# One transformer layer on eight cores: LayerNorm's small operations, a buffer of half the width, and a scheduler that weighs ScalarE's table loads more

## The chip, the cores and the metric

The kernel runs on all 8 cores of one Trainium2 chip. Each core does the same program on its own sequence (batch element) of 4096 tokens by 1024 features; the cores exchange nothing. The metric is the device time of the slowest core in microseconds (us). The kernel before took 1746.99 us, the median of three runs from 1746.04 to 1747.79.

A core has engines that run at the same time and wait for each other by semaphores: TensorE (PE) multiplies 128x128 blocks into eight PSUM banks, VectorE (DVE) and ScalarE (ACT) do elementwise work, GpSimd (POOL) does little here, and SyncE (SP) starts the transfers of x and y. Each engine takes its own instructions strictly in the order in which the program has them.

## What is computed

LN is LayerNorm without weights. Everything is along the 4096 tokens of one sequence:

```python
def attn(x):                                  # x = LN(input)
    xc = causal_depthwise_conv(x, conv_weight, conv_bias)     # 4 taps
    r = sigmoid(xc @ Wr.T + Wr_b);  i = sigmoid(xc @ Wi.T + Wi_b)
    a = power(sigmoid(log_a), 8 * r)
    b = sqrt(clip(1 - a * a, 1e-6)) * (i * xc)
    logA = clip(cumsum(log(clip(a, 1e-7))), -80)              # over tokens
    h = exp(logA) * cumsum(b * exp(-logA))                    # over tokens
    return rmsnorm(h @ out_w.T, norm_w)
def ffn(x):                                   # x = LN(input)
    xr = mu_r * x + (1 - mu_r) * x_prev;  xk = mu_k * x + (1 - mu_k) * x_prev
    return sigmoid(xr @ W_r.T) * (square(relu(xk @ W_k.T)) @ W_v.T)
x = x + LN(attn(LN(x)))
x = x + LN(ffn(LN(x)))
```

## The kernel before

**Chunks.** The tokens are worked in 16 chunks of 256. The first half of a chunk (F) loads it (L336), normalises it (statistics L443 to L475, L495), transposes it (L511, evacuated by ScalarE at L518), does the convolution as matmuls with diagonal matrices (L544, bias L553, evacuated L561), and computes the two gates: 64 matmuls with w_wr and 64 with w_wi (L586), each group of 8 into one PSUM bank, evacuated with Sigmoid (L595). The second half (B) of a chunk is the recurrence and the feed-forward part. In the program's loop the second half of chunk c-1 is emitted around the first half of chunk c, so that both stand in one period.

**The recurrence (B1).** z = r times a constant (L614, VectorE); la = max(z, clip) (L633); ScalarE computes exp(2z) (L637); VectorE clips it (L641); ScalarE takes sqrt(1 - that) (L653); VectorE scans la over the tokens in eight instructions (L666), adds the carry and clips (L678, eight), multiplies i by xc (L619) and that by the root (L657); ScalarE computes exp(-logA) (L688) and exp(logA) (L709); VectorE multiplies (L691), scans again (L700, eight) and forms h (L718, eight). Then h goes through w_ow (L758, 32 matmuls).

**The feed-forward part (B2).** Behind w_ow come RMS norm, LayerNorm, the residual (L770 to L825), the third LayerNorm (L841), transposes (L857, L864), the token mix (L883 to L899), r = Sigmoid(w_fr) (L919 matmuls, L927 ScalarE), k = Relu(w_fk) (L950 matmuls, L960 ScalarE), its square (L968, VectorE), w_fv (L988, 32 matmuls), the product with r (L996, VectorE, reads PSUM), the fourth LayerNorm, the residual (L1026), the store of y, and, behind that store on the same queue, the load of the chunk that reuses this input buffer.

**Buffers.** There are pools of buffers of 128x2048 elements: five of fp32 (`p32`) and six of bf16 (`p16`); a buffer is taken from a ring in the order of emission, and its new writer waits until its old readers are done. In listings both are shown as p. Six PSUM banks (PS) are taken in turn in the same way: a bank's next matmul group waits until ScalarE or VectorE has read the last one. PT is a seventh and eighth bank for transposes.

**What sets the order.** The program first emits all operations with their dependences and an estimated length, then `schedule()` lays them out with a list scheduler on estimated times. An operation's priority is the longest estimated path behind it, and of the ready operations of an engine the one with the highest priority goes first. On ScalarE `pick_scalar` takes up to 6 ready operations and adds TBL_NS (1283) to the priority of those whose table set is the one loaded: Exp and Ln are one set, Sigmoid another, Sqrt a third; Copy, Square and Relu run in any. The order that comes out is fixed in the program; on the chip no engine changes it.

## Time and profile before

| what | value |
|---|---|
| median of three runs | 1746.99 us |
| the profiled execution | 1742.71 us |
| its span, slowest core (core 1) | 1741.2 us (cores: 1720.7 to 1741.2) |
| PE busy | 983.3 us, 56% |
| DVE busy | 944.7 us, 54% |
| ACT busy | 816.4 us, 47% |
| the chain that ended last, by engine | PE 40%, DVE 24%, ACT 17%, issue 15% |
| mean granted TensorE clock, core 1 | 0.778 of full speed |

No engine is busy for more than 56% of the span. The chain that ended last follows the work backwards from the last instruction to what released it each time; it runs through three engines, so that the time is set by how they wait for each other. Busy shares are means over a period of some 102 us that repeats 15 times. Each line of a listing of instructions has its start in us from the start of the span, its length, the engine, the line of the kernel, output and input, the shape and how many were merged (xN), and in square brackets how long the engine had been idle and what released it.

### The profile page before, as it was taken

The numbers are of one execution on the slowest core, as the hardware profiler recorded it, in microseconds if no ns is written. First come the engines' busy times: TensorE is split into PE (matmuls) and PEld (weight loads), VectorE is DVE, ScalarE is ACT, GpSimd is POOL, SyncE is SP. The second block draws the span as 40 slices with busy tenths as digits, with TensorE's granted clock in tenths as the row PEclk, the third lists the DMA queues.
The fourth block names the chain that finished last, engine by engine and source line by source line (L and its number), as shares of the span: only waits on it lengthen the run. The fifth ranks groups of instructions, "written<-read, shape, count | busy, mean of one in ns | idle before, by whom it ended". The sixth has DMA issues, their size and how long they took to land.

```text
span 1741.2 us, 20480 instructions; the slowest of 8 cores (1720.7 to 1741.2 us)
## 1 busy us (share of the span) xinstructions
PE 983.3 (56%) x5762; PEld 595.8 (34%) x5762; DVE 944.7 (54%) x1570; ACT 816.4 (47%) x1303; POOL 30.8 (2%) x57
## 2 busy tenths in 40 slices
PE   0345737464664747467484656838465673846525
PEld 0133415142442515244251433416143341514313
DVE  0145565565456565555655555565555556555552
ACT  0554635354563535446354544635364463545422
POOL 1000000000000000000000000000000000000000
PEclk9977969687886867778686776868697786867867
DMA  9650010101001010000101000010100001010000
GB/s 131 123 85 1 1 49 1 49 1 39 10 1 49 1 49 1 31 19 1 49 1 49 1 25 25 1 49 1 49 1 25 25 1 49 1 48 1 1 24 25
DMA packets 21360, 47.49 MB, mean 27 GB/s; under 512 B 6912, under 2 KB 6912, under 8 KB 21248
## 3 DMA queue, kind: packets, MB, share of 16 engines
q1 hardware_dynamic: 14944, 33.59, 5.7%
q0 software_dynamic: 6304, 12.59, 4.8%
q8 instruction: 48, 0.79, 0.2%
q14 instruction: 64, 0.52, 0.1%
HBM read 41.99 MB, written 16.78 MB: 34 GB/s over the span
## 4 chain that ended last, share of the span: by engine, by line
PE 40%; DVE 24%; ACT 17%; issue 15%; SPq 2%; DMA 1%; DVEq 1%; ACTq 1%
PE PS L586 10%; PE PS L758 8%; PE PS L988 8%; PE PS L544 5%; DVE p L700 5%; PE PS L950 5%; ACT p L595 4%; DVE p L718 4%; ACT p L960 2%; DVE p L614 2%; DVE xin L1026 2%; ACT p L637 2%; ACT PS L455 2%; ACT p L709 2%; DVE vout L1019 2%
## 5 line engine op out<-in xcount | busy, mean ns | idle before, releaser
L758 PE MATMUL PS<-w_ow,p 128*128 128x512 bf16 x512 | 141.2, 444 | 331.8 <-DVE p L718 305.6
L758 PEld LDWEIGHTS PS<-w_ow,p 128*128 128x128 bf16 x512 | 56.8, 111 | 416.2 <-issue 373.0
L988 PE MATMUL PS<-w_fv,p 128*128 128x512 bf16 x512 | 150.0, 463 | 76.3 <-DVE p L968 43.5
L455 ACT ACTIVATE PS<-xin 128x1024 f32<-128x1024 f32 x64 | 65.8, 1028 | 263.7 <-DMA xin<-x 204.6
L544 PE MATMUL PS<-ln1F,diag 128*128 128x256 bf16 x512 | 108.6, 386 | 126.6 <-ACT stats L472 104.6
L586 PE MATMUL PS<-p,w_wi 128*128 128x256 bf16 x1024 | 149.2, 298 | 51.9 <-ACT p L595 51.7
L586 PE MATMUL PS<-p,w_wr 128*128 128x256 bf16 x1024 | 143.4, 305 | 25.8 <-ACT p L595 23.4
L919 PE MATMUL PS<-w_fr,p 128*128 128x512 bf16 x512 | 136.3, 391 | 9.9 <-DVE p L893 7.0
L586 PEld LDWEIGHTS PS<-p,w_wi 128*128 128x128 bf16 x1024 | 106.5, 106 | 95.1 <-issue 70.4
L586 PEld LDWEIGHTS PS<-p,w_wr 128*128 128x128 bf16 x1024 | 110.1, 109 | 56.2 <-issue 33.3
L950 PE MATMUL PS<-p,w_fk 128*128 128x256 bf16 x1024 | 123.4, 275 | 5.6 <-ACT p L595 3.2
L544 PEld LDWEIGHTS PS<-ln1F,diag 128*128 128x128 bf16 x512 | 65.1, 132 | 165.0 <-issue 142.0
L988 PEld LDWEIGHTS PS<-w_fv,p 128*128 128x128 bf16 x512 | 57.6, 114 | 168.6 <-issue 133.1
L950 PEld LDWEIGHTS PS<-p,w_fk 128*128 128x128 bf16 x1024 | 100.1, 99 | 28.2 <-issue 8.9
L614 DVE TENSOR_TENSOR p<-p,c_loga 128x2048 f32<-128x2048 bf16 x16 | 36.7, 2293 | 129.6 <-ACT p L595 129.6
L666 DVE TENSOR_TENSOR_SCAN p<-p,zeros 128x256 f32<-128x256 f32 x128 | 88.5, 692 | 13.6 <-DVE p L666 0.5
L700 DVE TENSOR_TENSOR_SCAN p<-p,zeros 128x256 f32<-128x256 bf16 x128 | 88.5, 692 | 13.2
L595 ACT ACTIVATE p<-PS,c_wrb 128x256 bf16<-128x256 f32 x128 | 60.7, 474 | 73.2 <-PE PS L586 64.1
L968 DVE TENSOR_TENSOR p<-p 128x2048 bf16<-128x2048 bf16 x16 | 19.6, 1225 | 118.3 <-ACT p L960 76.1
L770 ACT ACTIVATE vout<-PS 128x512 f32<-128x512 f32 x64 | 38.2, 597 | 75.4 <-PE PS L758 72.5
L595 ACT ACTIVATE p<-PS,c_wib 128x256 bf16<-128x256 f32 x128 | 60.7, 474 | 25.4 <-PE PS L586 16.2
L919 PEld LDWEIGHTS PS<-w_fr,p 128*128 128x128 bf16 x512 | 51.1, 100 | 58.2 <-issue 20.8
(99 smaller groups left out, 1484.2 us busy)
## 6 DMA issues: line engine op xcount, KB each, us to landing
xin<-x SPq DMA_DIRECT2D x16, 1024.0 KB, 6.1
y<-xin SPq DMA_DIRECT2D x16, 1024.0 KB, 4.2
w_wr<-wr POOLq DMA_DIRECT2D x1, 2048.0 KB, 19.9
w_wi<-wi POOLq DMA_DIRECT2D x1, 2048.0 KB, 30.5
w_ow<-ow POOLq DMA_DIRECT2D x1, 2048.0 KB, 41.8
w_fr<-fr POOLq DMA_DIRECT2D x1, 2048.0 KB, 18.2
w_fk<-fk POOLq DMA_DIRECT2D x1, 2048.0 KB, 29.9
w_fv<-fv POOLq DMA_DIRECT2D x1, 2048.0 KB, 22.1
```

The lines of the kernel that those rows point to most:

```text
L455: lambda e, s2=s, b=b, S_=S_, xap=xap, base=base: e.activation(bank2(b), xap[:, s2, :], AF.Square, bias=0.0, scale=1.0, accum_out=S_[:, ba ...
L544: lambda e, b=b, ch=ch, kk=kk, half=half: e.matmul(PS[:, b * 512 + half * CH: b * 512 + half * CH + CH], diag[:, ch * 4 + kk, :], ln1F[:, ...
L586: lambda e, b=b, wn=wn, k=k, m=m, xcF=xcF: e.matmul(bank(b, CH), wsb[wn][:, k, m * 128:(m + 1) * 128], feat(xcF)[:, k, :], start=(k == 0), ...
L595: lambda e, b=b, gb=gb, m=m, biasn=biasn: e.activation(feat(gb)[:, m, :], bank(b, CH), AF.Sigmoid, bias=cols[biasn][:, m:m + 1], scale=1.0),
L614: lambda e, z=z, r16=stt["r16"], bc=lnsig_bc: e.tensor_tensor(feat(z), feat(r16), bc, ALU.mult),
L666: lambda e, m=m, cb=cbuf, la=la: e.tensor_tensor_scan(feat(cb)[:, m, :], feat(la)[:, m, :], zeros32[:, :], 0.0, ALU.add, ALU.add),
L700: lambda e, m=m, S2=Ssc, t=tbuf: e.tensor_tensor_scan(feat(S2)[:, m, :], feat(t)[:, m, :], zeros32[:, :], 0.0, ALU.add, ALU.add),
L718: lambda e, m=m, h=hF, A=Abuf, S2=Ssc: e.scalar_tensor_tensor(feat(h)[:, m, :], feat(S2)[:, m, :], carryS[:, m:m + 1], feat(A)[:, m, :], A ...
L758: lambda e, b=b, k=k, s=s, half=half, hF=hF: e.matmul(bank(b), feat(hF)[:, k, s * 128:(s + 1) * 128], wsb["ow"][:, k, half * 512:(half + 1 ...
L919: lambda e, b=b, k=k, s=s, half=half, xr=xrF: e.matmul(bank(b), feat(xr)[:, k, s * 128:(s + 1) * 128], wsb["fr"][:, k, half * 512:(half + ...
L950: lambda e, b=b, k=k, m=m, half=half, xk=xkF: e.matmul(PS[:, b * 512 + half * CH: b * 512 + half * CH + CH], wsb["fk"][:, k, m * 128:(m + ...
L988: lambda e, b=b, k=k, s=s, half=half, ka=kaF: e.matmul(bank(b), feat(ka)[:, k, s * 128:(s + 1) * 128], wsb["fv"][:, k, half * 512:(half + ...
```

## The change

Four edits go together:

1. **LayerNorm statistics.** Before, the sum of squares was divided by D in its own VectorE instruction (L463) and the square of the mean subtracted from it in another (L469). Now one scalar_tensor_tensor does both.
2. **Table weight.** `pick_scalar` looks at 10 ready operations in place of 6 and gives 2600 in place of 1283 to those of the loaded set. The price of a load in the scheduler's own clock (TBL_NS) stays.
3. **Buffers.** Four fp32 and eight bf16 buffers in place of five and six: the same memory.
4. **r in bf16.** The result of L927, which L996 reads, is written to a bf16 buffer.

The other switches in the diff (PT1) are off and change nothing.

```diff
@@ -21,11 +21,13 @@
 SUB = CH // 128
 NXIN = int(os.environ.get("K_NXIN", "2"))
 NST = int(os.environ.get("K_NST", "4"))
-N_P32 = int(os.environ.get("K_P32", "5"))
-N_P16 = int(os.environ.get("K_P16", "6"))
+N_P32 = int(os.environ.get("K_P32", "4"))
+N_P16 = int(os.environ.get("K_P16", "8"))
 N_VOUT = int(os.environ.get("K_VOUT", "1"))
 BANK_MODE = os.environ.get("K_BANKS", "global")
 PT_ROLE = os.environ.get("K_PTROLE", "0") == "1"
+PT1 = os.environ.get("K_PT1", "0") == "1"
+RF16 = os.environ.get("K_RF16", "1") == "1"
 HOPX = float(os.environ.get("K_HOP", "250"))
 SQ2 = os.environ.get("K_SQ", "0") == "1"
 XFG = os.environ.get("K_XFG", "0") == "1"
@@ -56,6 +58,8 @@
 
 
 TBL_NS = 1283.0
+TBL_BONUS = float(os.environ.get("K_TBLNS", "2600"))
+TBL_WIN = int(os.environ.get("K_TBLWIN", "10"))
 COLD_IDLE = 800.0
 COLD_WIN = 3400.0
 
@@ -133,12 +137,12 @@
 
         def pick_scalar():
             tmp = []
-            while ready["scalar"] and len(tmp) < 6:
+            while ready["scalar"] and len(tmp) < TBL_WIN:
                 tmp.append(heapq.heappop(ready["scalar"]))
             best_key, best_adj = None, None
             for key in tmp:
                 op = self.all[key[-1]]
-                adj = -key[0] + (TBL_NS if (op.afn and op.afn == cur_tbl) else 0.0)
+                adj = -key[0] + (TBL_BONUS if (op.afn and op.afn == cur_tbl) else 0.0)
                 if best_adj is None or adj > best_adj:
                     best_adj, best_key = adj, key
             for key in tmp:
@@ -265,7 +269,7 @@
 
     sch = Sched()
     if BANK_MODE == "global":
-        banksF = banksM = banksB = Banks(0, 6)
+        banksF = banksM = banksB = Banks(0, 7 if PT1 else 6)
     else:
         banksF = Banks(0, 2)
         banksM = Banks(2, 2)
@@ -310,8 +314,8 @@
         vouts = [sb("vout%d" % i, [128, SUB * D], F32) for i in range(N_VOUT)]
         p32 = Pool([sb("p32_%d" % i, [128, SUB * D], F32) for i in range(N_P32)])
         p16 = Pool([sb("p16_%d" % i, [128, SUB * D], BF16) for i in range(N_P16)])
-        PS = st.enter_context(nc.psum_tensor("PS", [128, 3072], F32))
-        PT = st.enter_context(nc.psum_tensor("PT", [128, 2048], BF16))
+        PS = st.enter_context(nc.psum_tensor("PS", [128, 3584 if PT1 else 3072], F32))
+        PT = st.enter_context(nc.psum_tensor("PT", [128, 1024 if PT1 else 2048], BF16))
         tb_free = [[], []]
 
         def bank(b, n=512):
@@ -460,15 +464,13 @@
             tm_ = sch.emit("vector", lambda e, S_=S_, base=base: e.tensor_single_scalar(
                 S_[:, base + 4:base + 4 + SUB], S_[:, base:base + SUB], 1.0 / D, ALU.mult),
                 deps=t1, est=150)
-            te2 = sch.emit("vector", lambda e, S_=S_, base=base: e.tensor_single_scalar(
-                S_[:, base + 6:base + 6 + SUB], S_[:, base + 2:base + 2 + SUB], 1.0 / D, ALU.mult),
-                deps=tsq, est=150)
             tmm = sch.emit("vector", lambda e, S_=S_, base=base: e.tensor_tensor(
                 S_[:, base + 8:base + 8 + SUB], S_[:, base + 4:base + 4 + SUB], S_[:, base + 4:base + 4 + SUB], ALU.mult),
                 deps=[tm_], est=150)
-            tq = sch.emit("vector", lambda e, S_=S_, base=base: e.tensor_tensor(
-                S_[:, base + 8:base + 8 + SUB], S_[:, base + 6:base + 6 + SUB], S_[:, base + 8:base + 8 + SUB], ALU.subtract),
-                deps=[te2, tmm], est=150)
+            tq = sch.emit("vector", lambda e, S_=S_, base=base: e.scalar_tensor_tensor(
+                S_[:, base + 8:base + 8 + SUB], S_[:, base + 2:base + 2 + SUB], 1.0 / D,
+                S_[:, base + 8:base + 8 + SUB], ALU.mult, ALU.subtract),
+                deps=tsq + [tmm], est=150)
             tln = sch.emit("scalar", lambda e, S_=S_, base=base: e.activation(
                 S_[:, base + 14:base + 14 + SUB], S_[:, base + 8:base + 8 + SUB], AF.Ln, bias=LN_EPS, scale=1.0),
                 deps=[tq], est=250, afn="exp")
@@ -503,7 +505,7 @@
             tok_tr1 = []
             tok_ev1 = []
             for s2 in range(SUB):
-                tb = 0 if PT_ROLE else s2
+                tb = 0 if (PT1 or PT_ROLE) else s2
                 trs_ = []
                 for j in range(KC):
                     trs_.append(sch.emit(
@@ -849,7 +851,7 @@
             tok_evF = []
             tok_trF = []
             for s2 in range(SUB):
-                tb = 1 if PT_ROLE else s2
+                tb = 0 if PT1 else (1 if PT_ROLE else s2)
                 trs_ = []
                 for j in range(KC):
                     trs_.append(sch.emit(
@@ -904,7 +906,7 @@
                 "gpsimd", lambda e: e.tensor_copy(fF[:, :, 0:1], fF[:, :, CH:CH + 1]),
                 deps=[tok_d] + tok_xr + tok_xk + [glob["tok_tailF"]], est=400)
 
-            rf32, rfdep = p32.take()
+            rf32, rfdep = (p16.take() if RF16 else p32.take())
             tok_rf = []
             all_wr = []
             for s in range(SUB):
@@ -1004,7 +1006,7 @@
                     tok_vo.append(te)
                     banksB.give(ids, [te])
             p16.give(kaF, all_wv)
-            p32.give(rf32, tok_vo)
+            (p16 if RF16 else p32).give(rf32, tok_vo)
 
             acc4 = stats[:, ps, 64:64 + 2 * SUB].rearrange("p (a b) -> p a b", b=2)
             t1d = sch.emit("vector", lambda e, S_=S_, acc4=acc4: e.tensor_tensor(
```

The rows below are the programs' orders. The changed kernel's line numbers are 4 higher than before up to the LayerNorm statistics (L460 is L464) and 2 higher behind them (L586 is L588, L614 is L616); between, L466 is L467 and L469 is L470. A name such as p_3 is buffer 3 of one of the pools. All periods from the second to the last but one have the same rows but for the numbers of buffers and banks.

TensorE, in one period, from the transposes of the third LayerNorm (L857) to the first w_fk matmuls, before:

```order
L857 MATMUL PT<-ident,p_5 128x128 x16
L586 MATMUL PS<-p_3,w_wr 128x256 x64
L586 MATMUL PS<-p_3,w_wi 128x256 x26
L919 MATMUL PS<-w_fr,p_5 128x512 x2
L586 MATMUL PS<-p_3,w_wi 128x256 x4
L919 MATMUL PS<-w_fr,p_5 128x512 x2
L586 MATMUL PS<-p_3,w_wi 128x256 x2
L919 MATMUL PS<-w_fr,p_5 128x512 x11
L586 MATMUL PS<-p_3,w_wi 128x256 x10
L919 MATMUL PS<-w_fr,p_5 128x512
L586 MATMUL PS<-p_3,w_wi 128x256 x22
L950 MATMUL PS<-p_1,w_fk 128x256 x52
```

and in the changed kernel, the stretch with the last w_wr matmuls:

```order
L588 MATMUL PS<-p_3,w_wi 128x256 x2
L588 MATMUL PS<-p_3,w_wr 128x256 x2
L921 MATMUL PS<-w_fr,p_7 128x512 x2
L588 MATMUL PS<-p_3,w_wi 128x256 x2
L588 MATMUL PS<-p_3,w_wr 128x256 x2
L588 MATMUL PS<-p_3,w_wi 128x256 x2
L588 MATMUL PS<-p_3,w_wr 128x256 x2
L921 MATMUL PS<-w_fr,p_7 128x512 x2
L588 MATMUL PS<-p_3,w_wi 128x256 x2
L588 MATMUL PS<-p_3,w_wr 128x256 x2
L588 MATMUL PS<-p_3,w_wi 128x256 x4
L952 MATMUL PS<-p_0,w_fk 128x256
```

The gate matmuls with w_wr and w_wi stood one behind the other; now they are mixed two by two, with w_fr among them. Ahead of the last w_wr matmul stand 64 w_wr before, and 64 w_wr, 44 w_wi and 16 w_fr now.

ScalarE, from the first gate evacuation to the last Exp of the recurrence, before:

```order
L595 ACTIVATE p_5<-PS,c_wrb 128x256 x8
L595 ACTIVATE p_1<-PS,c_wib 128x256 x2
L637 ACTIVATE p_2<-p_1 128x2048
L595 ACTIVATE p_1<-PS,c_wib 128x256 x2
L927 ACTIVATE p_4<-PS 128x512 x2
L595 ACTIVATE p_1<-PS,c_wib 128x256 x4
L709 ACTIVATE p_1<-p_3 128x2048
L960 ACTIVATE p_1<-PS 128x512 x4
L927 ACTIVATE p_4<-PS 128x512 x2
L653 ACTIVATE p_3<-p_2 128x2048
L688 ACTIVATE p_5<-p_3 128x2048
```

and now, from the fifth w_wr evacuation on (ahead of these stand four of w_wr and two of w_wi):

```order
L597 ACTIVATE p_1<-PS,c_wrb 128x256 x2
L597 ACTIVATE p_5<-PS,c_wib 128x256 x2
L929 ACTIVATE p_2<-PS 128x512 x2
L597 ACTIVATE p_1<-PS,c_wrb 128x256 x2
L597 ACTIVATE p_5<-PS,c_wib 128x256 x2
L639 ACTIVATE p_1<-p_2 128x2048
L597 ACTIVATE p_5<-PS,c_wib 128x256 x2
L655 ACTIVATE p_6<-p_1 128x2048
L962 ACTIVATE p_1<-PS 128x512 x4
L929 ACTIVATE p_2<-PS 128x512 x2
L690 ACTIVATE p_7<-p_0 128x2048
L711 ACTIVATE p_1<-p_0 128x2048
```

The Sqrt (L653, now L655) has moved ahead of the Relu evacuations; Exp(logA) (L709, now L711), which stood ahead of them, is the last, behind Exp(-logA) (L688, now L690), with no other set between. The sets loaded in a period change seven times before and six times now.

VectorE, from z to the square of k, before:

```order
L614 TENSOR_TENSOR p_0<-p_1,c_loga 128x2048
L896 TENSOR_TENSOR p_1<-p_2,c_muk 128x2048
L899 TENSOR_TENSOR p_1<-p_1,fF 128x2048
L633 TENSOR_SCALAR p_1<-p_0 128x2048
L641 TENSOR_SCALAR p_3<-p_3 128x2048
L666 SCALAR_TENSOR_TENSOR p_4<-p_1,zeros 128x256 x8
L672 COPY ctmp<-p_4 128x8
L678 TENSOR_SCALAR p_4<-p_4,carryC 128x256
L619 TENSOR_TENSOR p_4<-p_0,p_3 128x2048
L678 TENSOR_SCALAR p_4<-p_4,carryC 128x256 x7
L683 TENSOR_TENSOR carryC<-carryC,ctmp 128x8
L968 TENSOR_TENSOR p_3<-p_0 128x2048
```

and now:

```order
L898 TENSOR_TENSOR p_0<-p_6,c_muk 128x2048
L901 TENSOR_TENSOR p_0<-p_0,fF 128x2048
L616 TENSOR_TENSOR p_2<-p_1,c_loga 128x2048
L635 TENSOR_SCALAR p_3<-p_2 128x2048
L643 TENSOR_SCALAR p_1<-p_1 128x2048
L668 SCALAR_TENSOR_TENSOR p_0<-p_3,zeros 128x256 x3
L621 TENSOR_TENSOR p_4<-p_5,p_3 128x2048
L668 SCALAR_TENSOR_TENSOR p_0<-p_3,zeros 128x256 x5
L674 COPY ctmp<-p_0 128x8
L970 TENSOR_TENSOR p_5<-p_1 128x2048
L680 TENSOR_SCALAR p_0<-p_0,carryC 128x256 x8
```

The mix for w_fk (L896, L899) now stands ahead of z. The square of k (L968, now L970) stands ahead of the eight carry additions (L678, now L680) and no longer behind them.

VectorE, around the product with r, before:

```order
L657 TENSOR_TENSOR p_4<-p_5,p_4 128x2048
L691 TENSOR_TENSOR p_4<-p_4,p_1 128x2048
L996 SCALAR_TENSOR_TENSOR vout,stats<-PS,p_2 128x512 x4
L1010 TENSOR_TENSOR stats<-stats 128x2
L460 TENSOR_SCALAR stats<-stats 128x2
L463 TENSOR_SCALAR stats<-stats 128x2
L466 TENSOR_TENSOR stats<-stats 128x2
L469 TENSOR_TENSOR stats<-stats 128x2
L700 SCALAR_TENSOR_TENSOR p_2<-p_4,zeros 128x256
L1019 TENSOR_SCALAR vout<-vout,stats 128x1024 x2
L1026 TENSOR_TENSOR xin<-xin,vout 128x2048
L700 SCALAR_TENSOR_TENSOR p_2<-p_4,zeros 128x256 x7
```

and now:

```order
L659 TENSOR_TENSOR p_4<-p_6,p_4 128x2048
L693 TENSOR_TENSOR p_4<-p_4,p_7 128x2048
L702 SCALAR_TENSOR_TENSOR p_2<-p_4,zeros 128x256 x2
L998 SCALAR_TENSOR_TENSOR vout,stats<-PS,p_2 128x512 x4
L1012 TENSOR_TENSOR stats<-stats 128x2
L464 TENSOR_SCALAR stats<-stats 128x2
L467 TENSOR_TENSOR stats<-stats 128x2
L470 SCALAR_TENSOR_TENSOR stats<-stats 128x2
L702 SCALAR_TENSOR_TENSOR p_2<-p_4,zeros 128x256
L1021 TENSOR_SCALAR vout<-vout,stats 128x1024 x2
L1028 TENSOR_TENSOR xin<-xin,vout 128x2048
L702 SCALAR_TENSOR_TENSOR p_2<-p_4,zeros 128x256 x5
```

Two of the eight second scans (L700, now L702) stand ahead of the product L998, and the LayerNorm statistics have three instructions instead of four, with one instead of three behind ScalarE's squares.

## Rows read from the trace of the kernel before

**Rows 1.** By stage: length; PE, PEld, DVE, ACT, POOL busy (instructions); PE clock; DMA share, GB/s:

```profile
1456.00:1464.50 8.50, 8.47 (x36) 3.73 (x37) 4.89 (x9) 3.40 (x11) 0.00 (x0) 0.83 0.00 0
1464.50:1486.00 21.50, 11.56 (x72) 7.48 (x70) 10.55 (x27) 12.41 (x27) 0.22 (x1) 0.61 0.01 2
1486.00:1528.40 42.40, 32.34 (x227) 22.90 (x224) 24.16 (x28) 23.81 (x33) 1.22 (x1) 0.90 0.00 1
1528.40:1538.30 9.90, 9.77 (x32) 3.62 (x32) 2.92 (x3) 6.77 (x5) 0.00 (x0) 0.72 0.00 0
1538.30:1558.60 20.30, 0.01 (x1) 0.04 (x1) 16.53 (x33) 3.74 (x8) 0.00 (x0) 0.56 0.29 103
```

**Rows 2.** TensorE's instructions in time, first w_ow of the program:

```profile
137.91 8.73 PE L758 MATMUL PS<-w_ow,p 128*128 128x512 bf16 x32 [26.20 <-DVE stats L463]
```

**Rows 3.** TensorE's instructions in time, last w_ow of the program:

```profile
1660.84 8.44 PE L758 MATMUL PS<-w_ow,p 128*128 128x512 bf16 x32 [20.36 <-DVE p L718]
```

**Rows 4.** Who waited for whom: us in total, times, longest:

```profile
PE PS L758 <- DVE p L718: 305.6, 15, 20.6
```

**Rows 5.** ScalarE's table loads (112, six groups): busy us, mean ns | idle before:

```profile
L595 ACT ACT_TABLE_LOAD x32 | 41.1, 1283 | 28.7 <-PE PS L586 27.3
...
L709 ACT ACT_TABLE_LOAD x15 | 19.2, 1283 | 89.6 <-DVE p L678 89.6
```

**Rows 6.** ScalarE's instructions in time, gate stage of that period:

```profile
1501.78 1.28 ACT L637 ACT_TABLE_LOAD   x1 [1.46 <-DVE p L614]
1503.07 1.91 ACT L637 ACTIVATE p<-p 128x2048 f32<-128x2048 f32 x1
...
1520.17 1.28 ACT L709 ACT_TABLE_LOAD   x1 [6.25 <-DVE p L678]
...
1523.46 2.67 ACT L960 ACTIVATE p<-PS 128x512 bf16<-128x512 f32 x4
...
1527.50 1.29 ACT L927 ACTIVATE p<-PS 128x512 f32<-128x512 f32 x2
```

**Rows 7.** ScalarE's instructions in time, when the next x has come:

```profile
1557.57 1.03 ACT L455 ACTIVATE PS<-xin 128x1024 f32<-128x1024 f32 x1 [13.80 <-DMA xin<-x]
```

**Rows 8.** VectorE's instructions in time, same period:

```profile
1499.35 2.29 DVE L614 TENSOR_TENSOR p<-p,c_loga 128x2048 f32<-128x2048 bf16 x1 [6.46 <-ACT p L595]
...
1508.14 6.25 DVE L666 TENSOR_TENSOR_SCAN p<-p,zeros 128x256 f32<-128x256 f32 x8
...
1526.98 1.23 DVE L968 TENSOR_TENSOR p<-p 128x2048 bf16<-128x2048 bf16 x1 [6.68 <-ACT p L960]
...
1537.84 0.69 DVE L996 SCALAR_TENSOR_TENSOR vout<-PS,p 128x512 f32<-128x512 f32 x1 [1.09 <-PE PS L988]
...
1545.86 2.29 DVE L1026 TENSOR_TENSOR xin<-xin,vout 128x2048 f32<-128x2048 f32 x1
1548.25 5.46 DVE L700 TENSOR_TENSOR_SCAN p<-p,zeros 128x256 f32<-128x256 bf16 x7
1553.83 4.61 DVE L718 SCALAR_TENSOR_TENSOR p<-p,carryS,p 128x256 bf16<-128x256 f32 x8
```

**Rows 9.** TensorE's instructions in time, first gate matmuls of that period:

```profile
1486.05 4.28 PE L586 MATMUL PS<-p,w_wr 128*128 128x256 bf16 x22
...
1492.07 4.64 PE L586 MATMUL PS<-p,w_wr 128*128 128x256 bf16 x41 [0.30 <-ACT p L595]
```

**Rows 10.** TensorE's instructions in time, its wait in the gates, and on:

```profile
1506.97 0.37 PE L586 MATMUL PS<-p,w_wi 128*128 128x256 bf16 x1 [2.67 <-ACT p L595]
...
1520.66 2.75 PE L919 MATMUL PS<-w_fr,p 128*128 128x512 bf16 x12
1528.47 9.77 PE L988 MATMUL PS<-w_fv,p 128*128 128x512 bf16 x32 [5.05 <-DVE p L968]
```

**Rows 11.** VectorE's groups by line: count | busy us, mean ns | idle before:

```profile
L678 DVE TENSOR_SCALAR p<-p,carryC 128x256 f32<-128x256 f32 x128 | 45.2, 353 | 15.9 <-DVE p L678 2.8
...
L463 DVE TENSOR_SCALAR stats<-stats 128x2 f32<-128x2 f32 x64 | 10.8, 169 | 52.1 <-ACT PS L455 50.6
```

## The prediction

> **What bounds the kernel now.** I read the shares of the page first: no engine is busy for more than 56% of the span, so no sum of busy times gives the end. The chain of waits runs through three engines. The table by stage shows a period of 102.6 us in five stages [rows 1]: w_ow on TensorE (8.5), a stage of norms and convolution (21.5), gates, w_fr and w_fk (42.4), w_fv (9.9), and 20.3 us in which TensorE does nothing and VectorE is busy for 16.5. The list of waits names that last gap: TensorE waited for h (L718) 15 times, 305.6 us in all [rows 4]. From the first to the last w_ow there are 15 periods, (1660.84 - 137.91)/15 = 101.5 us each [rows 2, 3]; whatever shortens a period counts 15 times.
>
> Within a period I then read the timelines of the three engines, from the gates on [rows 6, 8 to 10]. z (L614) starts at 1499.35, when w_wr's eight banks are evacuated. The first scans (L666) start at 1508.14 and the carry additions (L678) end at 1520.0, for on ScalarE the load for Exp(logA) (L709) starts at 1520.17. The Relus (L960) stand behind it and start at 1523.46, though the w_fk matmuls were done at 1520.6 (there the last twelve of w_fr start). Behind them the square (L968) comes at 1526.98, w_fv at 1528.47, and the product L996 at 1537.84, 9.37 us into w_fv. From L996 VectorE works almost without a break to the end of L718 at 1558.44. So two things decide a period: when L996 can start, and how much VectorE still has to do after it.
>
> **The change part by part.** Times are in that period, as if all ahead of the gates stayed.
>
> *Gates.* The first TensorE matmuls go as before: 22 in 4.28 us, 0.195 each, then at the higher rate 41 in 4.64 us, 0.113 each [rows 9]; a 512-column matmul takes 0.23 (2.75/12) [rows 10] and counts as two units. At 1492.07 some 28 of the new order are done (26 of w_wr and two of w_wi, whose banks came free at the same moment as now). The last w_wr is number 64 + 44 + 2x16 = 140. 112 units x 0.113 = 12.7, so it ends at 1504.7. ScalarE then has two evacuations of w_fr and two of w_wr, 2.1 us with their gaps: z starts at 1507.05, **7.7 us later** than before.
>
> *From z to the scans.* Before, the mix for w_fk (3.5 us and gaps) stood between z and L633; it now lies in VectorE's wait ahead of z and costs nothing. Then z 2.29, load 1.28 and Exp 1.91 on ScalarE [rows 6], the clip 1.23, hops of 0.15 to 0.2 each: the scans start at 1514.25, 6.1 later than before. Eight scans with L619 among them and L672 take 6.25 + 1.33 + 0.28 and gaps, to 1522.2.
>
> *w_fk.* Before, TensorE waited 2.67 us at unit 126 for ScalarE, which was inside Exp(2z) and its two loads, and went on at 1506.97 [rows 10]. In the new order a like wait (the banks of the last w_wr and w_wi) comes at unit 145 and ends near 1508.1, with some 150 done where the old order had 131. That is 19 units, 2.2 us: w_fk ends at 1518.4 in place of 1520.6.
>
> *ScalarE.* After Exp(2z), a load and two w_wi evacuations the Sqrt takes 1.28 + 1.91 to 1518.4; the Relus follow at once, to 1521.3, as nothing of L709 (1.28 + 1.91) stands ahead of them. w_fr's evacuations with their load end at 1524.0.
>
> *Square and w_fv.* L968 starts behind the scans at 1522.3 and ends at 1523.5; w_fv needs also w_fr's last bank: it starts at 1524.1, 4.3 earlier. Its 9.37 us to the first product give 1533.5.
>
> *VectorE up to the product.* The eight carry additions, 8 x 0.35 and gaps 3.7 [rows 11], end at 1527.3; load and Exp(-logA) to 1530.6; L691 and two scans to 1533.7. So VectorE and TensorE arrive together, and L996 starts at 1533.8, **4.0 us earlier**. Exp(logA) runs beside it. The two engines are within 0.3 us of each other: half a gain on one is no gain.
>
> *After the product.* Two of eight scans are done already: 2 x 0.8 = **1.6** (5.46 for seven, and gaps) [rows 8]. The LayerNorm: of three instructions behind ScalarE's squares one is left, the other moves into the wait; 2 x 0.27 = **0.5** (0.17 each and the gap) [rows 11]. No row has a scalar_tensor_tensor of two columns; L996, of 512, takes 0.69, at most what it costs [rows 8], and at least the 0.17 of the tensor_scalar. Nearest in size is the latter, which I take. In the other three LayerNorms of a period the same 0.5 lies beside other work of ScalarE or TensorE (the transpose's evacuation, the convolution, the first part of w_ow) and I count nothing; without that cover it would be 0.5 x 3 more gained, not lost.
>
> *r in bf16.* ScalarE writes 512 columns in 0.6 to 0.7 us as bf16 (L960, 2.67 for four) and as fp32 (L927, 1.29 for two) alike [rows 6]. VectorE's scans with a bf16 input take 5.46 for seven against 6.25 for eight in fp32, the same each [rows 8]. So nothing; the bounds are 0.1 either way for four products.
>
> *The table load.* The 112 loads of 1.28 us [rows 5] become some 97; of the one saved per period the worth is already in the above, since L709 no longer stands ahead of the Relus.
>
> *The buffers.* With four fp32 buffers Exp(logA) must write where the Sqrt read. That is why the Sqrt has to come first; it stands first, so no wait is left of it.
>
> *The x transfer.* The store of y goes out at the end of L1026 (1548.15) and x is there at 1557.57, 9.4 later [rows 7, 8]. Five scans and h are 8.7 us now, so the first norm's statistics wait for x 0.7 us more; w_ow (8.4 us) covers that and the statistics with about 1 us left.
>
> Sum: 4.0 + 1.6 + 0.5 = 6.1 in this period. It is one of the better: where TensorE's clock stays low for longer after its wait, w_fk ends later and the gain is nearer to 5. I take 5.5 x 15 = 82. The first chunk, with its Sqrt ahead of six w_wi evacuations, may lose 1.7; the last one, with three LayerNorms in the open, gains 1.6. From the profiled execution's 1742.7: 1660.7. The median of the runs is 4.3 above that execution, so 1665.
>
> Here a rule speaks about price. From the end of the Relus (1526.13) to the start of w_fr's evacuation (1527.50) the rows show 1.37 us, with one load of 1.28 in it [rows 5, 6]. The Trainium skill, ScalarE: Activation LUTs, section What ACT_TABLE_LOAD costs, adds a drain of about 1380 ns to each switch, 2.66 us in all; by it the load taken from ahead of the Relus would be worth 1.4 us more a period, about 20 us more in all. The trace does not agree, and I leave it out.
>
> **Rivals.** *z is later still.* The mixing of w_wi into w_wr is paid in z. If TensorE's clock falls in the mixed stretch (the low level costs 0.195 in place of 0.113 a matmul), 40 units at it put z 3.3 us later, VectorE decides alone, and a period gains 2.8: 42 in all, 1705. For it: VectorE is already on the edge. Against it: the same matmuls ran at 0.113 for 41 in a row [rows 9].
>
> *The x transfer becomes the bound.* The margin is some 1 us. If the transfer takes 2.5 us longer against other cores' traffic, since it starts under more load, a period loses 1.5 of its 5.5: 60 in all, 1687.
>
> *The order of before was the better.* The square now stands in VectorE's queue ahead of the carry additions. If w_fk ended late, it would hold them, Exp(-logA) and the scans. Its place is L968, its price each us that w_fk is late. From w_fk's end to the product it takes 15.1 us now and took 17.2 before (1537.84 - 1520.6); with the 2.1 after the product the change loses only if w_fk ends over 4.2 us later than before. Twice the wait of 2.67 and 20 units more at the low rate (1.6) would do that just about; at 5 us late it is 0.8 x 15 = 12 slower, 1759. Nothing in the rows shows it.
>
> *Only the loads count.* If the reordering cancels itself and only 0.5 us of the norm is won in a period, it is 8 us, 1739.
>
> **How the numbers follow.** The forecast, a gain of 4.5 to 6.5 a period, 0.58; z later 0.16; the x transfer 0.10; nearly nothing won 0.09, a third of it within 0.2%; slower 0.04; a clock that stays high in more places, a gain of 7 to 8 a period, 1635, 0.03. The range: below, the last case and a w_fk end that lets 7 us be won; above, z later with its 1705 and a little more. 1638 to 1708. A difference under 0.2% (3.5 us) can't be told from none with this kernel. Faster 0.93, within 0.2% 0.03, slower 0.04.
>
> **What would show it.** In the profile after: z should start some 7 to 8 us later in the period than now; VectorE's wait ahead of the square should be nearly gone; w_fv should begin about 4 us earlier and wait for w_fr's last bank or the square; the first product should find two scans done; Exp(logA) should run with no load ahead of it; loads should number some 97; TensorE's wait for h should fall from 20.35 to about 18.5. The prediction is wrong if the gates' stage does not end earlier, or if w_ow begins to wait for x or for buffers; if the span falls by less than 40 us, the step on z is the first to suspect.

## The result, and the profile after

The changed kernel takes 1641.87 us (median; 1635.57 to 1643.55) where the kernel before took 1745.43 in the same comparison: a ratio of 0.9401, 95% interval 0.9387 to 0.9416, 103.6 us less. Measured again on another chip it was 1638.65 us against 1742.2, 0.9406 (0.9386 to 0.9426). The forecast was 1665 with a range of 1638 to 1708; the time came out 23 us below it, 4 us above the range's lower end.

The page of the changed kernel: the span, busy times, and the shares of the chain that ended last.

```profile
span 1640.9 us, 19943 instructions; the slowest of 8 cores (1627.7 to 1640.9 us)
...
PE 947.8 (58%) x5762; PEld 583.2 (36%) x5762; DVE 934.2 (57%) x1506; ACT 795.9 (49%) x1287; POOL 15.7 (1%) x57
...
PE 34%; DVE 32%; ACT 15%; issue 13%; SPq 2%; DMA 1%; DVEq 1%; ACTq 1%
```

VectorE has come up to TensorE, and in the chain of waits it has nearly TensorE's share. By stage, the period that begins at 992.15, with the columns of [rows 1]:

```profile
992.00:1000.50 8.50, 8.35 (x32) 3.57 (x33) 4.91 (x9) 4.08 (x10) 0.00 (x0) 0.82 0.01 2
1000.50:1022.20 21.70, 11.82 (x74) 7.77 (x73) 10.21 (x25) 12.56 (x27) 0.23 (x1) 0.61 0.00 0
1022.20:1059.40 37.20, 30.87 (x226) 22.36 (x224) 21.29 (x20) 24.05 (x33) 0.22 (x1) 0.95 0.01 1
1059.40:1068.20 8.80, 8.75 (x32) 3.48 (x32) 5.66 (x11) 5.20 (x4) 0.00 (x0) 0.81 0.00 0
1068.20:1088.00 19.80, 0.09 (x1) 0.10 (x1) 16.27 (x31) 2.71 (x7) 0.00 (x0) 0.55 0.27 106
```

Four of the five stages are within 1.1 us of those before. The gates' stage is 37.2 us in place of 42.4, with TensorE granted 0.95 of its clock in place of 0.90. TensorE's timeline of that period shows a part of it: the one wait of 2.67 us in the gates of [rows 10] has become three short ones, here 0.95 and two of 0.30 (only the first is shown). All waits from the first gate matmul to w_fk's end are 2.5 us in place of 5.1. Then come the last of w_fr, w_fv, and w_ow of the next period; below them the last w_ow of the program, which answers to [rows 3].

```profile
1042.16 0.27 PE L588 MATMUL PS<-p,w_wi 128*128 128x256 bf16 x1 [0.95 <-ACT p L597]
...
1052.90 2.75 PE L921 MATMUL PS<-w_fr,p 128*128 128x512 bf16 x12
1059.44 8.75 PE L990 MATMUL PS<-w_fv,p 128*128 128x512 bf16 x32 [3.79 <-DVE p L970]
1087.91 8.43 PE L760 MATMUL PS<-w_ow,p 128*128 128x512 bf16 x32 [19.72 <-DVE p L720]
```

```profile
1559.15 10.02 PE L760 MATMUL PS<-w_ow,p 128*128 128x512 bf16 x32 [16.99 <-DVE p L720]
```

From the first w_ow (139.13) to the last are 15 periods in 1420.0 us, 94.67 each, against 101.53 before [rows 2, 3]: 6.86 x 15 = 103 us, the whole gain. The list of waits answers to [rows 4]:

```profile
PE PS L760 <- DVE p L720: 290.4, 15, 20.1
```

290.4/15 = 19.4 us a period in place of 20.4, where the prediction had 18.5. VectorE's timeline from z on, to be read beside [rows 8]:

```profile
1042.76 2.29 DVE L616 TENSOR_TENSOR p<-p,c_loga 128x2048 f32<-128x2048 bf16 x1 [9.99 <-ACT p L597]
...
1048.56 1.23 DVE L643 TENSOR_SCALAR p<-p 128x2048 f32<-128x2048 f32 x1 [2.18 <-ACT p L639]
1049.89 2.28 DVE L668 TENSOR_TENSOR_SCAN p<-p,zeros 128x256 f32<-128x256 f32 x3
...
1057.95 1.22 DVE L970 TENSOR_TENSOR p<-p 128x2048 bf16<-128x2048 bf16 x1 [0.21 <-DVE ctmp L674]
...
1066.37 1.22 DVE L693 TENSOR_TENSOR p<-p,p 128x2048 bf16<-128x2048 bf16 x1 [2.18 <-ACT p L690]
1067.70 1.49 DVE L702 TENSOR_TENSOR_SCAN p<-p,zeros 128x256 f32<-128x256 bf16 x2
1069.29 0.69 DVE L998 SCALAR_TENSOR_TENSOR vout<-PS,p 128x512 f32<-128x512 f32 x1
...
1073.87 0.16 DVE L470 SCALAR_TENSOR_TENSOR stats<-stats 128x2 f32<-128x2 f32 x1 [0.66 <-ACT PS L459]
...
1083.15 4.62 DVE L720 SCALAR_TENSOR_TENSOR p<-p,carryS,p 128x256 bf16<-128x256 f32 x8
1088.15 2.29 DVE L447 TENSOR_REDUCE stats<-xin 128x2 f32<-128x2048 f32 x1 [0.39 <-DMA xin<-x]
```

z (L616) has a wait of 9.99 us ahead of it; the square (L970), which waited 6.68, waits 0.21; the product (L998) has no wait ahead of it. The end of L720 releases w_ow. From z to the end of L720 VectorE has two more waits of 2.18 us for ScalarE, which then works on what VectorE has just made (Exp(2z) and Exp(-logA)), and one of 0.66. So the chain from z on is VectorE's own work with these stops. x is there at 1088.1, 0.2 us after w_ow has begun. ScalarE, beside [rows 6]:

```profile
1045.18 1.28 ACT L639 ACT_TABLE_LOAD   x1 [1.46 <-DVE p L616]
...
1052.17 1.91 ACT L655 ACTIVATE p<-p 128x2048 bf16<-128x2048 f32 x1
1054.17 2.67 ACT L962 ACTIVATE p<-PS 128x512 bf16<-128x512 f32 x4
...
1058.21 1.29 ACT L929 ACTIVATE p<-PS 128x512 bf16<-128x512 f32 x2
...
1066.29 1.91 ACT L711 ACTIVATE p<-p 128x2048 f32<-128x2048 f32 x1
```

The Sqrt (L655) comes first, the Relus (L962) follow it, and Exp(logA) (L711) has no load ahead. Of loads there are 99: 32 by L597, 16 each by L639, L655, L690 and L929, and three at the program's ends (the 112 of before leave those three out). Three of the groups, beside [rows 5]:

```profile
L597 ACT ACT_TABLE_LOAD x32 | 41.1, 1283 | 26.8 <-PE PS L588 25.4
...
L655 ACT ACT_TABLE_LOAD x16 | 20.5, 1283 | 5.5 <-DVE p L621 3.0 <-DVE p L643 1.5
L690 ACT ACT_TABLE_LOAD x16 | 20.5, 1283 | 50.4 <-DVE p L680 50.4
```

To compare kernels I read the same moments off the timelines of each of the core that the profile shows and took means over periods 2 to 14 (us; "gates" is the first gate matmul, "product" the first L996 or L998). The runs of the experiments stand in the same table:

```
                    w_ow to  gates   w_fk end  gates    gates to  product to  period
                    gates    to z    (from g.) to w_fv  product   next w_ow
before              29.51    13.05   34.59     42.13    51.31     20.77       101.59
after               29.22    20.03   30.57     36.87    46.70     18.70        94.63
e1_ln_only          29.26    13.30   34.80     42.20    51.61     20.45       101.32
e2_buf_only         29.02    20.25   30.55     36.96    46.89     19.27        95.18
e3_tbl_old          28.78    20.03   30.57     36.83    46.67     18.70        94.15
e4_p16_6            28.74    12.92   35.68     41.84    50.70     17.98        97.42
e6_delay            29.12    20.15   30.57     36.92    46.82     18.70        94.63
e7_wr_first         37.87    13.19   33.53     38.93    47.72     17.04       102.63
e8_residual_pool    37.76    19.82   30.73     36.75    46.46     20.27       104.49
e9_wr_first_head    29.06    13.12   33.28     38.90    47.78     17.09        93.92
e10_head_only       36.65    20.33   30.63     37.12    47.00     18.67       102.32
e11_norm_scalar     28.54    20.24   30.60     37.01    46.91     18.07        93.52
e12_both            29.26    13.30   33.24     39.03    47.90     16.50        93.66
```

### The profile page after: what moved, and what is told of

It is laid out like the page before. It is cut to its first block, busy times and chain, and to the rows that moved or that the text cites. A ratio compares the mean times of both kernels' runs of the same rounds, so it can differ in the third digit from the quotient of the medians.

```text
span 1640.9 us, 19943 instructions; the slowest of 8 cores (1627.7 to 1640.9 us)
## 1 busy us (share of the span) xinstructions
PE 947.8 (58%) x5762; PEld 583.2 (36%) x5762; DVE 934.2 (57%) x1506; ACT 795.9 (49%) x1287; POOL 15.7 (1%) x57
## 4 chain that ended last, share of the span: by engine, by line
PE 34%; DVE 32%; ACT 15%; issue 13%; SPq 2%; DMA 1%; DVEq 1%; ACTq 1%
PE PS L588 11%; PE PS L760 9%; PE PS L546 6%; DVE p L702 5%; DVE p L668 5%; DVE p L720 4%; PE PS L921 4%; DVE p L680 3%; ACT p L597 2%; DVE xin L1028 2%; DVE p L616 2%; ACT p L690 2%; ACT p L639 2%; DVE vout L1021 2%; ACT PS L459 2%
## 5 line engine op out<-in xcount | busy, mean ns | idle before, releaser
L760 PE MATMUL PS<-w_ow,p 128*128 128x512 bf16 x512 | 147.1, 459 | 320.5 <-DVE p L720 290.4
L588 PE MATMUL PS<-p,w_wi 128*128 128x256 bf16 x1024 | 182.2, 274 | 33.8 <-ACT p L597 33.6
L588 PE MATMUL PS<-p,w_wr 128*128 128x256 bf16 x1024 | 179.3, 301 | 3.7 <-ACT p L563 2.4
L990 PE MATMUL PS<-w_fv,p 128*128 128x512 bf16 x512 | 143.5, 449 | 62.9 <-DVE p L970 53.0
L546 PE MATMUL PS<-ln1F,diag 128*128 128x256 bf16 x512 | 103.9, 373 | 126.1 <-ACT stats L474 120.7
L952 PE MATMUL PS<-p,w_fk 128*128 128x256 bf16 x1024 | 141.8, 275 | 9.0 <-ACT p L597 5.5
L616 DVE TENSOR_TENSOR p<-p,c_loga 128x2048 f32<-128x2048 bf16 x16 | 36.7, 2293 | 176.1 <-ACT p L597 176.1
L588 PEld LDWEIGHTS PS<-p,w_wi 128*128 128x128 bf16 x1024 | 99.4, 98 | 73.6 <-issue 46.5
L588 PEld LDWEIGHTS PS<-p,w_wr 128*128 128x128 bf16 x1024 | 109.4, 108 | 33.4 <-issue 4.8
L597 ACT ACTIVATE p<-PS,c_wrb 128x256 bf16<-128x256 f32 x128 | 60.7, 474 | 74.0 <-PE PS L588 66.4
L702 DVE TENSOR_TENSOR_SCAN p<-p,zeros 128x256 f32<-128x256 bf16 x128 | 88.6, 692 | 13.9 <-DVE p L702 0.9
L447 DVE TENSOR_REDUCE stats<-xin 128x2 f32<-128x2048 f32 x16 | 36.6, 2286 | 61.1 <-DMA xin<-x 61.0
L720 DVE SCALAR_TENSOR_TENSOR p<-p,carryS,p 128x256 bf16<-128x256 f32 x128 | 62.0, 484 | 14.6 <-DVE p L702 0.7
L597 ACT ACTIVATE p<-PS,c_wib 128x256 bf16<-128x256 f32 x128 | 60.7, 474 | 11.6 <-PE PS L588 1.2
```

Of the source, the lines that this page charges most:

```text
L546: lambda e, b=b, ch=ch, kk=kk, half=half: e.matmul(PS[:, b * 512 + half * CH: b * 512 + half * CH + CH], diag[:, ch * 4 + kk, :], ln1F[:, ...
L588: lambda e, b=b, wn=wn, k=k, m=m, xcF=xcF: e.matmul(bank(b, CH), wsb[wn][:, k, m * 128:(m + 1) * 128], feat(xcF)[:, k, :], start=(k == 0), ...
L597: lambda e, b=b, gb=gb, m=m, biasn=biasn: e.activation(feat(gb)[:, m, :], bank(b, CH), AF.Sigmoid, bias=cols[biasn][:, m:m + 1], scale=1.0),
L616: lambda e, z=z, r16=stt["r16"], bc=lnsig_bc: e.tensor_tensor(feat(z), feat(r16), bc, ALU.mult),
L702: lambda e, m=m, S2=Ssc, t=tbuf: e.tensor_tensor_scan(feat(S2)[:, m, :], feat(t)[:, m, :], zeros32[:, :], 0.0, ALU.add, ALU.add),
L720: lambda e, m=m, h=hF, A=Abuf, S2=Ssc: e.scalar_tensor_tensor(feat(h)[:, m, :], feat(S2)[:, m, :], carryS[:, m:m + 1], feat(A)[:, m, :], A ...
```

## Experiments

Each ratio is to the kernel before on the same chip, with its 95% interval.

**Which part pays: e1 to e4.** The first takes the kernel before and changes the LayerNorm's variance alone.

```diff
-            te2 = ... tensor_single_scalar(S_[:, base+6..], S_[:, base+2..], 1.0 / D, ALU.mult)
-            tq = ... tensor_tensor(S_[:, base+8..], S_[:, base+6..], S_[:, base+8..], ALU.subtract)
+            tq = ... scalar_tensor_tensor(S_[:, base+8..], S_[:, base+2..], 1.0 / D,
+                     S_[:, base+8..], ALU.mult, ALU.subtract)
```

> The kernel before with the LayerNorm edit alone; the order of all else stays. Theory (only the fourth LayerNorm of a period stands on the path, 2 x 0.27 us): about 0.53 x 15 = 8 us faster than before plus some 1.6 in the last chunk, 1745 to 1736, ratio 0.995. Rival (all four LayerNorms of a period stand on the path): 0.53 x 4 x 15 = 32 us, 1713. Rival (the new instruction costs what its neighbours saved): no change.

Measured: 1732.35 us, 0.9927 (0.9904 to 0.9949), 12.7 us less, where the expectation had some 10. Its 15 periods take 7.5 us less, 0.5 each, which is the number predicted, but in part by luck: behind the product, where the theory puts the gain, the table has 0.32 (20.45 for 20.77), and over all eight cores a period is 0.37 shorter. The last chunk, from the last w_ow on, is 4.1 us shorter (76.3 in place of 80.4), for 1.6 expected.

The second takes the kernel before with the buffers alone.

```diff
-N_P32 = 5; N_P16 = 6;  rf32, rfdep = p32.take()
+N_P32 = 4; N_P16 = 8;  rf32, rfdep = p16.take()
```

> The kernel before with the four fp32 and eight bf16 buffers and r in bf16, but the old LayerNorm and the old table weight. Theory (the buffers alone make the new order, the rest of the gain is theirs): changed kernel plus the LayerNorm's 9 to 10 us, 1642 + 9 = 1651. Rival (the table weight does a good part of it): 1665 or more, and seven loads a period.

Measured: 1646.1 us, 0.9427 (0.9406 to 0.9447). The first theory holds: the buffers alone bring the new order and 6.4 of the 7.0 us a period; the LayerNorm adds 0.57 behind the product (19.27 to 18.70).

The third takes the table edit out of the changed kernel: TBL_BONUS 1283 and TBL_WIN 6.

> The changed kernel with the table weight of before (6 ready operations, 1283). The steady periods come out in the same order. Theory (the table weight changes next to nothing here): 1642, within 2 us. Rival (it saves the load of each period, 1.28 us): 1642 + 19 = 1661.

Measured: 1629.86 us, 0.9338 (0.932 to 0.9355): faster than the changed kernel, whose two intervals it does not touch, and outside both expectations. e2 and e3 differ in the LayerNorm alone: 1646.1 and 1629.86, 16 us on the same chip. So of the change's parts the buffers give most, the LayerNorm 13 to 16 us, and with the table edit the kernel is some 11 us slower. The steady periods are ordered alike in e3 and the changed kernel. Two things differ. In the last chunk the larger weight lets one Relu stand behind w_fr's last evacuation, to save a load. ScalarE's timelines there, the changed kernel and then this one:

```profile
1610.59 1.98 ACT L962 ACTIVATE p<-PS 128x512 bf16<-128x512 f32 x3 [7.65 <-PE PS L952]
1613.29 1.29 ACT L929 ACTIVATE p<-PS 128x512 bf16<-128x512 f32 x2 [0.73 <-PE PS L921]
1614.67 0.60 ACT L962 ACTIVATE p<-PS 128x512 bf16<-128x512 f32 x1
```

```profile
1601.86 2.66 ACT L962 ACTIVATE p<-PS 128x512 bf16<-128x512 f32 x4 [7.65 <-PE PS L952]
1604.62 1.29 ACT L929 ACTIVATE p<-PS 128x512 bf16<-128x512 f32 x2
```

The last twelve w_fr matmuls start at 1610.60 and at 1601.87; with the Relu held back w_fv starts 6.32 us behind that, without it 4.31, and the first product 14.38 and 11.32. So the table edit costs 3.1 us in the last chunk: 2.0 by w_fv's later start, 1.1 by w_fv itself, whose 32 matmuls take 8.46 us in place of 7.07 (81.8 us from the last w_ow on in the changed kernel, 76.4 here; the other 2.3 are w_ow and w_fr at different clocks). The second part lies in the lengths of single periods: the 15 of them take 1409.2 us in the mean over the eight cores, and 1414.1 in the changed kernel. e5 and e6 take that up.

The fourth takes two of the eight bf16 buffers away again: N_P16 = 6.

> The changed kernel with four fp32 and six bf16 buffers: Sqrt and Relus stand ahead of Exp(logA), as in the changed kernel, but the gate matmuls with w_wr and w_wi are not mixed and z is early, as before. Theory (half of the gain is that nothing stands ahead of the Relus, half that TensorE has no single long wait in the gates, which also keeps its clock up): w_fk ends as late as before, 34.6 us into the gates, the product comes some 49.5 us into the gates (51.3 before, 46.7 in the changed kernel), a period of about 98 us, 1690. Rival (the early z is worth more than the mixing): faster than the changed kernel, under 1640. Rival (the mixing is all): near before less the LayerNorm, 1735.

Measured: 1686.98 us, 0.9651 (0.9628 to 0.9675), near the theory's 1690, with the product at 50.7 us for its 49.5. By the table the stretch behind the product is the shortest of these four (17.98), and the product stands 4.0 us later than with eight. So the gain has two sources: four fp32 buffers with r in bf16 let scans go ahead of the product, and the seventh and eighth bf16 buffer bring the product forward.

**Chance or phase: e5 and e6.** e5 is the changed kernel again; e6 adds four redundant ScalarE activations in the first chunk.

```diff
+        for _ in range(4):
+            tok_diag[31] = sch.emit("scalar", lambda e: e.activation(
+                diag[:, 31, :], ident[:, :], AF.Copy, bias=0.0, scale=wconv[:, 7, 3:4]),
+                deps=[tok_diag[31]], est=300)
```

> The changed kernel itself, again, beside the kernel before, as the comparison for the three other kernels of this group. Theory: nothing changes; some 1641 us where the kernel before takes 1746 (ratio 0.940, 0.9387 to 0.9416 in its first runs). It also settles the difference to the version with the table weight of before, which had a ratio of 0.9338 (0.932 to 0.9355). Theory A, that the two differ by the phase in which the first chunk leaves the convolution of each period to TensorE's clock: the ratio stays near 0.940, and period by period the gap lies between the first gate matmul and the next w_ow's start nowhere, but in the stretch from the first gate matmul's w_ow to the gates (29.2 us in the changed kernel, 28.8 in the other). Theory B, that it was chance from one chip to another: the ratio comes out between 0.932 and 0.936.

> The changed kernel with four activations more on ScalarE in the first chunk, which write a diagonal block of the convolution again, the same values; some 2 us of ScalarE's work (four of 0.3 to 0.5 us), ahead of the periods; from the first w_ow on, the order of every engine is as in the changed kernel. Theory A (the start of the periods decides at which clock the convolution of each period runs, and that is what sets the changed kernel 0.7% above the version with the table weight of before): the time moves by something other than the added work, to between 1630 and 1650 us, and by 15 times a change of the stretch from w_ow to the gates (29.22 us now). Theory B (the steady state forgets its start): the time is that of the changed kernel plus 0 to 2 us, 1641 to 1644, and the stretch stays at 29.2 us within 0.05.

Measured: 1638.65 us, 0.9406 (0.9386 to 0.9426), and 1644.83 us, 0.9444 (0.9429 to 0.9459). So e3's lead is no chance of the chip. The lengths of the first ten periods, one by one:

```
after, core 4           95.5 95.9 94.8 96.7 92.9 94.0 96.0 93.5 93.6 95.8
after, core 5           93.0 94.0 96.3 95.1 93.3 94.1 93.3 94.2 93.0 93.1
e5_after_again, core 4  95.6 95.9 94.8 96.7 92.9 94.0 96.0 93.5 93.6 93.2
e5_after_again, core 7  92.9 94.0 96.2 95.1 93.3 94.1 93.3 94.3 93.0 93.1
e6_delay, core 1        95.5 95.9 93.9 94.2 94.5 93.6 94.5 95.6 95.6 95.6
e6_delay, core 5        95.6 95.9 93.8 94.2 94.5 93.7 94.5 95.6 95.7 95.6
```

The cores follow a few fixed sequences, the same on two chips, and the delay leads them into others. In the mean over the cores the first w_ow of e6 is 2.0 us later than in e5, and its 15 periods take 1418.3 us in place of 1413.7. So Theory B falls: the steady state does not forget its start. Theory A holds, though within the low end of what it allowed, 0.3% of the time. What differs most from period to period is the head (27.8 to 30.7 us in the changed kernel, in one order); from the gates to the next w_ow it is 64.1 to 66.1. Two heads of one profile (e11), whole, with the columns of [rows 1]:

```profile
889.05:916.54 27.49, 16.99 (x104) 9.69 (x105) 15.12 (x34) 16.59 (x37) 0.22 (x1) 0.81 0.02 7
981.62:1011.69 30.07, 20.17 (x104) 11.32 (x105) 15.13 (x34) 16.68 (x37) 0.23 (x1) 0.67 0.01 5
```

The same 104 matmuls, at 0.81 and at 0.67 of the clock: 27.5 and 30.1 us. Why a delay leads to one sequence of clocks and not another is not shown.

**Is the mixing of the gates what pays: e7 and e9.** e7 makes w_wi wait for w_wr's matmuls.

```diff
                             deps=tok_xcF + wcast[wn] + bdeps + prev
+                                 + (all_gate_mm[:KC] if wn == "wi" else []),
```

> The changed kernel, but each period's w_wi matmuls wait until w_wr's first blocks are all through, so that z is made early, as before the change, and still all buffers, the bf16 r and the LayerNorm are as after it. It undoes the mixing of the two gates alone. Theory A (the mixing is a price that the change pays in z, and what wins the time is the square, w_fv and the scans; VectorE decides up to the product): z starts some 6 to 7 us earlier than now after the gates' start (13.5 in place of 20.0), but the Sqrt, and with it the Relus and w_fk, come no earlier; the product starts 49.4 us after the gates in place of 46.7 and the scans done by then are more, so the stretch behind it falls to 17.2 from 18.7: a period of 95.8, 1660 us. Rival B (the mixing is immaterial, both orders end at the same VectorE work): as the changed kernel, 1636 to 1646 us. Rival C (z early is worth what it gains, 6 us in the scans, and VectorE has slack up to the product): a period of 91 to 92, 1590 to 1605 us.

Measured: 1755.73 us, 1.0076 (1.0056 to 1.0096), outside all three expectations. From the gates to the next w_ow it took 64.8 us, 0.6 less than the changed kernel. The loss is in the head, 37.9 in place of 29.2, which the edit does not touch, in 14 of 15 periods (the first has 28.5). In the head, the norm of the next x (L474 and L477 on ScalarE, L497 on VectorE) had moved behind w_ow's evacuation. The planner counts 5000 ns for the store of y and as many for the load of x. My reading, which e9 and e10 try: with z early its w_ow comes sooner, x seems late to it, and it puts other work first.

e9 is e7 with the assumed duration of these transfers changed, which touches no instruction, only their order:

```diff
-  ... est=5000)      # the load of x (two places) and the store of y
+  ... est=4000)
```

> The kernel with w_wr's matmuls first (e7_wr_first), with one number changed: the duration that the planner assumes for a transfer of x or y is 4000 ns in place of 5000. By it the order of the head of a period becomes again that of the changed kernel: the norm of the next x (its logarithm and exponential on ScalarE and the two L497) stands ahead of w_ow's evacuation and not behind it. The gates stay as in e7, w_wr first, z early. In e7 a period from the first gate matmul to the next w_ow took 64.75 us (47.72 + 17.04), less than the changed kernel's 65.4 (46.7 + 18.7), but the stretch from w_ow to the gates took 37.9 in place of 29.2, except in the first period (28.5). Theory A (what e7 lost was the order in the head alone, which the planner moved because it thought x late; the mixing of the gates itself is worth nothing): the head is 29.2 to 30.0 again, a period 94.0 to 94.8, the time 1626 to 1640 us. Rival B (x does come late, some 2.5 us after w_ow's start, since only three scans and h stand between the store of y and w_ow; the head waits for x whatever its order): 31 to 32 us of head, a period of 96.5, 1665 us. Rival C (the mixing of the gates is what pays): 1740 to 1756 us.

Measured: 1628.06 us, 0.9319 (0.9285 to 0.9354), a head of 29.06. Theory A. w_wr first or mixed, it is 64.9 or 65.4 us from the gates to w_ow: the mixing, on which the prediction spent most of its working, gains nothing. And x does come late in e9, as VectorE and TensorE show:

```profile
1086.24 2.29 DVE L447 TENSOR_REDUCE stats<-xin 128x2 f32<-128x2048 f32 x1 [2.84 <-DMA xin<-x]
```

```profile
1083.55 8.34 PE L761 MATMUL PS<-w_ow,p 128*128 128x512 bf16 x32 [16.63 <-DVE p L721]
1091.73 1.25 PE L513 MATMUL PT<-ident,p 128*128 128x128 bf16 x16
```

x is there 2.7 us after w_ow's start, and the transposes (L513) still follow w_ow without a wait. Over all eight cores they wait in 7 of the 112 heads from the second period on, by 1.2 us at most.

**The head alone: e10.** The changed kernel with est=6000 in the same three places.

> The changed kernel with that one number at 6000 ns in place of 5000: gates, scans, products and buffers are ordered as in the changed kernel, and only the norm of the next x moves behind w_ow's evacuation, as in e7_wr_first. Theory A (the order of the head is worth 8.6 us a period, by w_ow's evacuation and the four L794 that then stand ahead of the two L497 and so of the transposes and the convolution): a head of 37 to 38 us in 14 periods, a period of 103.3, 1641 + 14 x 8.6 = 1761 us. Rival B (the loss in e7 came from x's lateness, and here x is there 0.4 us after w_ow's start as in the changed kernel): a head of under 31 us, 1641 to 1665 us.

Measured: 1749.02 us, 1.0016 (1.0006 to 1.0027): the whole gain is gone. Gates, product and the stretch behind it are as in the changed kernel. TensorE's timeline in the head:

```profile
1052.31 9.95 PE L760 MATMUL PS<-w_ow,p 128*128 128x512 bf16 x32 [19.73 <-DVE p L720]
1070.93 1.01 PE L513 MATMUL PT<-ident,p 128*128 128x128 bf16 x8 [8.67 <-DVE p L497]
1076.91 1.01 PE L513 MATMUL PT<-ident,p 128*128 128x128 bf16 x8 [4.97 <-DVE p L497]
```

Where the transposes had followed w_ow at once, they wait 8.67 and 4.97 us for L497. The head is 7.4 us longer in 14 periods, 104 us. Theory A, at 7.4 in place of its 8.6, so 12 us below its 1761.

**Less for VectorE behind the product: e8, e11, e12.** e8 gives the residual L1028 to GpSimd.

```diff
-            tok_xf = sch.emit("vector", ...
+            tok_xf = sch.emit("gpsimd", ...
```

> The changed kernel with the residual addition (y = x + v * w, L1028, 1024 columns fp32, one to two us of VectorE in each period) done by GpSimd in place of VectorE. It takes work off VectorE behind the product, where theory A says VectorE decides: from the product to w_ow is 18.70 us now, and it would be 16.3 without the 2.39 us of L1028. Theory A: this stretch gets shorter by 0.5 to 2.4 us a period, less what the x transfer loses, since GpSimd does the addition more slowly (estimate 2 to 4 us) and the store of y and the load of x start that much later; with some 1 us of margin left for x about 0.7 us a period remain, 1631 us (1605 to 1641). Rival B (x was at its margin, so each us that y is late is an us of w_ow or of the next norm): slower by 1 to 3 us a period, 1656 to 1686. Rival C (GpSimd's addition slows VectorE's scans beside it): the five scans from 0.80 us each to over 0.95, and no gain, 1641 to 1650.

Measured: 1783.91 us, 1.0242 (1.0223 to 1.026). VectorE and GpSimd in that stretch:

```profile
1059.79 7.91 DVE L702 TENSOR_TENSOR_SCAN p<-p,zeros 128x256 f32<-128x256 bf16 x5
```

```profile
1060.02 4.75 POOL L1028 TENSOR_TENSOR xin<-xin,vout 128x2048 f32<-128x2048 f32 x1 [52.24 <-DVE vout L1021]
```

Five scans take 7.91 us beside GpSimd's addition of 4.75, and 3.87 without it (L702 in the changed kernel): 4.04 us lost, most of the addition's length. One scan alone, the second (1060.59 to 1065.32), has all of it: 4.73 us, where the four others take 0.69 each. The Trainium skill, SBUF — State Buffer, section SBUF: two separate sides, says that the two engines share a pair of ports as an exclusive lock, in which a VectorE instruction with two SBUF inputs takes part against a GpSimd one that reads SBUF, and that the loser waits for the whole instruction. The trace agrees: the second scan, which began inside the addition (1060.02 to 1064.77), ended 0.55 us behind it, and the last three came after. Removing 2.39 us of VectorE's work made the stretch 1.6 longer. This is Rival C, with a price well beyond the one that I had put on it; the time lies outside all three expectations. The planner took x for late as well, so the rest, 8.5 us a period, is the head again (the first period, whose x is there from the start, has 29.2).

e11 gives VectorE's scaling in that norm to ScalarE.

```diff
+            tok_nb = ... vector scalar_tensor_tensor: S[54..] = (mean * -1) * rstd
-                    "vector", ... tensor_scalar(vout_s, vout_s, mean_s, rstd_s, subtract, mult)
+                    "scalar", ... activation(vout_s, vout_s, AF.Identity,
+                        bias=S_[:, 54 + s:55 + s], scale=S_[:, 58 + s:59 + s])
-            tok_xf = ... vector tensor_tensor(xb, xb, vout, ALU.add)
+            for s in range(SUB):  tok_xf = ... vector tensor_tensor(xb_s, xb_s, vout_s, ALU.add)
```

> The changed kernel with the last norm's two subtract-and-scale instructions (L1021, 1.73 us on VectorE, of vout) done by ScalarE as Identity with a scale and a bias of one value per partition; VectorE computes the bias (one instruction of two columns, 0.16) and adds the residual in two halves in place of one. ScalarE does nothing else there (it waits 13.4 us for x). Theory A (VectorE decides from z's start to w_ow: from the product to w_ow it has 18.7 us of work in a row): 1.83 less, 0.27 and 0.17 more, so 1.4 us less a period, 21 in all: a stretch from the product to w_ow of 17.3 and 1620 us (1612 to 1628). Rival B (y's store comes no earlier, and x, which lies at its margin, gives the time back in the head): the stretch falls to 17.3 but the head grows by 1.4: 1641 us. Rival C (the two hops to ScalarE and back stand in the chain to y, with too few scans to cover them): the stretch stays at 18.3 to 18.7, 1635 to 1645 us.

Measured: 1621.89 us, 0.9292 (0.9275 to 0.9308), the lowest median of all. VectorE:

```profile
1064.73 0.16 DVE L1017 SCALAR_TENSOR_TENSOR stats<-stats 128x2 f32<-128x2 f32 x1
1064.99 0.69 DVE L702 TENSOR_TENSOR_SCAN p<-p,zeros 128x256 f32<-128x256 bf16 x1
1066.46 2.56 DVE L1032 TENSOR_TENSOR xin<-xin,vout 128x1024 f32<-128x1024 f32 x2 [0.77 <-ACT vout L1024]
```

The time is Theory A's, the reason only half so. The stretch is 18.07, not 17.3, since one more wait of 0.77 us for ScalarE stands in it; 0.63 x 15 = 9 us. The head gives as much again (28.54 in place of 29.22), where the order is the same and only the clock's sequence is another; that half is luck.

e12 is e9 and e11 together.

> The two edits that gained, together: w_wr's matmuls first with the head's order kept (e9_wr_first_head) and the last norm's scaling on ScalarE (e11_norm_scalar). Theory A (the gains are on different stretches and add up: e9 took the gates' stage into account, e11 the stretch behind the product): 1628 - 20 = 1608 us (1600 to 1616), a ratio of 0.921. Rival B (x is now the bound: only two scans and h stand between the store of y and w_ow, so x comes 3 to 4 us after w_ow's start, and the norm, the transposes and the convolution with it): the head grows from some 29 to 31 us, and the time is no better than e11's, 1620 to 1632 us.

Measured: 1626.37 us, 0.9316 (0.9243 to 0.9389): the time of Rival B. Where the two edits act, their gains do add up: from the gates to the next w_ow the table has 65.40 us for the changed kernel, 64.87 for e9, 64.98 for e11 and 64.40 for both together. Theory A had added all 20 us of e11, half of which lay in the head's clock. In the head at 1067.19 x comes 3.6 us after w_ow's start, and the transposes still start 8.9 us after it, at w_ow's end:

```profile
1070.79 2.29 DVE L447 TENSOR_REDUCE stats<-xin 128x2 f32<-128x2048 f32 x1 [3.74 <-DMA xin<-x]
```

```profile
1067.19 9.04 PE L761 MATMUL PS<-w_ow,p 128*128 128x512 bf16 x32 [17.70 <-DVE p L721]
1076.07 1.13 PE L513 MATMUL PT<-ident,p 128*128 128x128 bf16 x16
```

In the head at 1255.31 x is 4.3 us late, and they wait:

```profile
1259.57 2.29 DVE L447 TENSOR_REDUCE stats<-xin 128x2 f32<-128x2048 f32 x1 [4.40 <-DMA xin<-x]
```

```profile
1255.31 8.85 PE L761 MATMUL PS<-w_ow,p 128*128 128x512 bf16 x32 [15.98 <-DVE p L721]
1264.45 0.61 PE L513 MATMUL PT<-ident,p 128*128 128x128 bf16 x8 [0.29 <-DVE p L497]
1265.37 0.61 PE L513 MATMUL PT<-ident,p 128*128 128x128 bf16 x8 [0.31 <-DVE p L497]
```

Whole, this head and one at 787.86, whose x is 3.2 us late, with the columns of [rows 1]:

```profile
787.86:815.31 27.45, 17.00 (x105) 9.72 (x106) 14.96 (x33) 16.51 (x37) 0.22 (x1) 0.81 0.08 28
1255.31:1286.45 31.14, 20.80 (x104) 11.31 (x105) 14.96 (x33) 16.63 (x37) 0.22 (x1) 0.66 0.10 31
```

What keeps e12 from Theory A's 1608 are these heads of two kinds, nine of 27.5 to 28.9 us and six of 30.5 to 31.2, and the spread of the cores: 1599 to 1620 us, of which the slowest is the time. The six are those whose x is 3.85 us late or more; from the second period on none of the others has it later than 3.60. Over all eight cores, of the 22 heads with x 3.6 us late or more, 20 take over 30.4 us, and of the 90 others one takes over 30. So Rival B holds in part: x is the bound in the heads in which it is later than some 3.6 us. Only 0.3 to 1.2 us of each of the six is the transposes' wait; most of the rest is TensorE at the lower clock (0.66 for 0.81). That the late x brings the clock down is only argued, for the changed kernel, whose x is never over 2.1 us late, also has heads up to 30.7 us.

The interval of e12 holds e9 and e11, so no order among the three is shown. e3, e9 and e11 are faster than both kernels by their intervals; that of e12 just meets the changed kernel's.

## Why the prediction was right, and where its sizes were off

The change was faster for the reason given in outline: an earlier product and less of VectorE's work behind it. But the gain of 6.9 us a period lies between two of its cases (4.5 to 6.5, and 7 to 8) and in neither, and what it said of x's margin and of the cause of the earlier product does not hold (the last two points).

- *z later by 7.7.* 7.0 (20.03 for 13.05), and the square's wait is gone as said. This is the mis-sized step that reached the time. The last w_wr matmul ended 17.9 us behind the first gate matmul (16.9 to 18.5) where the working had 18.65, and z came 2.1 behind that in place of 2.35.
- *w_fv 4.3 earlier, L996 4.0 earlier.* 5.3 and 4.6. From z to the product it takes 26.5 or 26.9 us in every period but the last (30.1), as the 7.7 and 4.0 of the prediction imply (38.3 - 11.7 = 26.6); with z 0.7 sooner than worked out, the product is 0.6 sooner.
- *w_fk's end 2.2 earlier.* It is 4.0 (30.57 for 34.59), the largest miss in size. I had put a wait like the old one of 2.67 us into the new order; there are three short ones of 1.55 us in all. All waits up to w_fk's end are 2.6 us less; the other 1.4 us are matmuls at a higher clock (0.95 for 0.90 in the gates' stage). It did not set the product: L998 has no wait ahead of it, so VectorE came last there.
- *Two scans ahead of the product and 0.5 of the LayerNorm, 2.1.* 2.07. e2 and the changed kernel give the second part 0.57, e1 0.32.
- *The LayerNorm in all.* 0.5 x 15 and 1.6 in the last chunk are 9 us. It is worth 12.7 (e1) and 16 (e3 against e2). What it gives beside the stretch behind the product, where I had counted nothing, lies in the last chunk (4.1 us in e1) and in heads whose clock is another; the two are not told apart further.
- *The sum.* 4.6 + 2.07 + 0.29 in the head = 6.96 a period by the table, 6.86 over all 15, for 6.1 worked out and 5.5 taken. The shading, for a clock that stays low behind TensorE's wait, was on the wrong side: 0.6 x 15 = 9 us; the product was 0.6 earlier than worked out, another 9.
- *First chunk 1.7 later, last 1.6 sooner.* The first w_ow is 1.2 later; but from the last w_ow on it takes 81.8 us in place of 80.4, of which e3 puts 3.1 on the table edit's Relu. So from the profiled 1742.7: less 6.86 x 15 = 102.9, and 2.6 for both ends, is 1642.4, as profiled; 4.9 of the 23 us are the medians' distance from the profiled runs.
- *r in bf16 costs nothing.* L998 takes 0.69 us as L996 did. The scalar_tensor_tensor of two columns, taken at 0.17, takes 0.16 (L470).
- *Some 97 loads said.* 96 without the three at the program's ends, at 1.28 us each. The load costs its own length: from L655's end (1054.08) to L962 0.09 us, from L962's end (1056.84) over a load to L929's start (1058.21) 1.37. The drain of some 1380 ns a switch that the Trainium skill, ScalarE: Activation LUTs, section What ACT_TABLE_LOAD costs, adds is not in it, and the forecast was right to leave those 20 us out.
- *The x transfer as the bound, 1687.* It was not the bound here: x is 0.2 us late in the period shown. I had counted about 1 us left beyond a lateness of 0.7, and that margin was too small: an x up to 3.6 us after w_ow's start costs nothing in e12. Beyond that the bound does come, in six of e12's heads. What x's lateness costs besides is indirect and larger: a planner that believes in it moves the norm, and that is 7.4 us a period (e10). At that price the rival would have read 1749, no change.
- *Reordering of the gates, and Exp(logA) no longer ahead of the Relus, as the source of the earlier product.* Only argued, and not so. e9 has w_wr first and is no slower. e9 also has Exp(logA) (712) with its load ahead of the Relus (963), as before the change, and the product at 47.8 us; e4 has it behind them, and the product at 50.7. Nor does the number of loads order the times: e4 has 84 and takes 1687 us, e9 has 127 and takes 1628. What the fast orders share is where ScalarE does the Sqrt. Its order in one period, by line, from z's Exp on (L637 or L639, the first in each row; Sqrt is L653, L655 or L656):

```
before   637  595x2 927x2 595x4  709  960x4 927x2  653  688
after    639  597x2  655  962x4 929x2  690 711
e9       640  930x2 598x2  656  598x2  712  963x4 930x2  691
e4       639  597x6 929x2 962x3 929x2 962  655  690 711
```

The kernel before and e4 do it last, ahead of Exp(-logA) (L688, L690), and have the product at 51.3 and 50.7 us; the two others do it ahead of the Relus and have 46.7 and 47.8. That this is the cause fits all four, but no run moved the Sqrt alone, so it is not shown and stays open.

## What to carry to other kernels

Where a planner orders the work, a resource edit (here two buffers more of one kind and one fewer of another) acts through the order; compare the order of every stage, also of those that the edit does not touch, before trusting a gain or a loss. The durations that the planner assumes for transfers are part of the kernel: one number changed by 20% gave back the whole 6%. Before pricing an order in detail, ask which engine has no wait left in the new one (here VectorE, from z to w_ow, but for its stops at ScalarE) and count its chain first. And do not take the number of table loads for time: e4, with 84 of them, was slower by 59 us than e9, with 127.

## What the runs showed of the hardware

- A GpSimd tensor_tensor in fp32 (4.75 us, 2048 columns) stopped VectorE's scan beside it: 4.73 us for one in place of 0.69, and 7.91 us for five in place of 3.87 (e8).
- TensorE's granted clock was 0.67 in one head and 0.81 in another of the same order, and the same work took 30.1 and 27.5 us (e11); in e12 it was 0.66 and 0.81, 31.1 and 27.5 us. Cores of two chips went through the same sequence of period lengths, within 0.1 us for nine periods, and some 2 us of work in the first chunk led them into others. Two kernels with one steady order differed by 4.6 us over the 15 periods in the mean of the cores (e5 and e6).
- ScalarE's Identity with a scale and a bias per partition takes 2.58 us for two of 1024 fp32 columns, where VectorE's subtract-and-scale takes 1.73.
